# The last layer of a four-layer graph network: two matrix products folded, one residual product moved into the units, normalisation steps re-placed

## What is computed

```python
def _L3_gnn_ref(h, adj, W, a, W_res, gamma, beta):
    Wh = h @ W
    src = Wh @ a[:F_OUT]
    dst = Wh @ a[F_OUT:]
    e = jax.nn.leaky_relu(src[:, :, None] + dst[:, None, :], ALPHA)
    e = jnp.where(adj > 0, e, NEG_INF)
    attention = jax.nn.softmax(e, axis=-1)
    h_prime = jnp.einsum('bij,bjf->bif', attention, Wh)
    h_prime = h_prime + h @ W_res
    h_prime = jax.nn.elu(h_prime)
    mean = jnp.mean(h_prime, axis=-1, keepdims=True)
    var = jnp.var(h_prime, axis=-1, keepdims=True)
    return (h_prime - mean) * jax.lax.rsqrt(var + LN_EPS) * gamma + beta
```

## Time and profile before

| | us |
|---|---|
| three runs, lowest, median, highest | 3643.5, 3647.93, 3651.93 |
| the profiled execution | 3658.79 |
| its span, first to last instruction | 3656.9 |
| of it the last layer, from 3264.1 | 392.8 |

### The profile page before, as it was taken

How to read it: one execution, slowest core, us unless ns; L and a number is a source line. 1 busy time by engine, 2 the same in 40 slices (tenths; PEclk the granted TensorE clock), 3 DMA queues, 4 the chain that set the end, 5 groups by cost and what they waited for, 6 DMA issues and landing times. The chain is left out here.

```text
span 3656.9 us, 79212 instructions
## 1 busy us (share of the span) xinstructions
PE 3145.9 (86%) x31515; PEld 1741.2 (48%) x31515; DVE 3129.5 (86%) x4797; ACT 2982.5 (82%) x3625; POOL 1005.0 (27%) x565
## 2 busy tenths in 40 slices
PE   7996998999999869889898898988988989968885
PEld 5663666666666633333333333333333333336764
DVE  6665887888888779999999999999999999956666
ACT  5664887887788759999999999999999999956555
POOL 4432655655566610100000000000010000016554
PEclk9997999999999989999999999999999999988788
DMA  6540000000000000000000000000000000001111
GB/s 229 207 141 16 22 16 19 19 19 19 19 19 19 22 7 10 10 10 10 10 10 12 11 10 10 10 10 10 10 10 10 10 10 10 13 17 57 51 52 35
DMA packets 67251, 110.62 MB, mean 30 GB/s; under 512 B 25941, under 2 KB 25944, under 8 KB 66904
## 3 DMA queue, kind: packets, MB, share of 16 engines
q1 hardware_dynamic: 66904, 105.77, 9.3%
HBM read 86.87 MB, written 18.87 MB: 29 GB/s over the span
## 5 line engine op out<-in xcount | busy, mean ns | idle before, releaser
L980 ACT ACTIVATE l_scalar_ring<-l_w,l_r 128x1024 f32<-128x1024 f32 x1632 | 1712.9, 1141 | 34.8 <-DVE l_values L1026 25.7
L1094 DVE TENSOR_SCALAR l_vector_ring<-l_w_code,l_r_code 128x2048 f32<-128x2048 f32 x1232 | 1588.9, 1354 | 3.1 <-issue 0.2
L917 PE MATMUL scores<-l_scalar_ring,l_signs 128*32 128x512 f32 x6528 | 792.0, 604 | 91.2 <-ACT l_scalar_ring L980 90.9
L927 PE MATMUL scores<-l_vector_ring,l_signs_code 128*32 128x512 f16 x9856 | 670.9, 393 | 140.1 <-DVE l_vector_ring L1094 139.3
L242 ACT COPY probs_t<-turned 128x512 f32<-128x512 f32 x576 | 324.7, 587 | 422.5 <-PE turned L201 422.3
L433 POOL TENSOR_TENSOR l_masked<-l_relu,mask 128x1024 f32<-128x1024 f32 x256 | 546.2, 2134 | 438.0 <-ACT l_relu L585 397.1
L927 PEld LDWEIGHTS scores<-l_vector_ring,l_signs_code 128*32 128x32 bf16 x9856 | 243.1, 95 | 592.1 <-DVE l_vector_ring L1094 308.8
L212 PE MATMUL outT<-probs_t,l_values 128*64 128x128 f32 x6144 | 433.9, 284 | 88.3 <-ACT probs_t L242 40.3
L212 PEld LDWEIGHTS outT<-probs_t,l_values 128*64 128x64 f32 x6144 | 343.1, 140 | 234.2 <-DVE l_acc L667 104.4
L269 ACT ACTIVATE l_probs<-l_logits,negmax 128x1024 f32<-128x1024 f32 x384 | 443.7, 1155 | 6.6 <-DVE negmax L260 6.6
L201 PE MATMUL turned<-ident,l_probs 128*128 128x128 f32 x3072 | 436.6, 287 | 12.1 <-issue 7.3
(11 more groups left out here) (239 smaller groups left out, 3148.1 us busy)
## 6 DMA issues: line engine op xcount, KB each, us to landing
mask<-masks_kept SPq DMA_DIRECT2D x192, 256.0 KB, 2.6
l_adj<-adj SPq DMA_DIRECT2D x64, 512.0 KB, 5.6
masks_kept<-l_mask_ring SPq DMA_DIRECT2D x64, 256.0 KB, 4.2
x_res<-x SPq DMA_DIRECT2D x8, 256.0 KB, 5.1
out<-x_res SPq DMA_DIRECT2D x8, 256.0 KB, 2.8
l_w_both<-L_gnn_Wq SPq DMA_DIRECT2D x2, 64.0 KB
l_w_both<-L_gnn_Wk SPq DMA_DIRECT2D x2, 64.0 KB
l_w_both<-L_gnn_Wv SPq DMA_DIRECT2D x2, 64.0 KB
```

Source lines behind the costliest of these rows:

```text
L917: last = nc.tensor.matmul(s.scores[g * ROWS:(g + 1) * ROWS, buf, half, :], signs[:, window], scalar_ring[:, at % SCALAR_RING, g, halves[ha ...
L927: last = nc.tensor.matmul(s.scores[g * ROWS:(g + 1) * ROWS, buf, half, :], signs_code[:, par, g % 2, window], parts(vector_ring[:, at % VE ...
L980: last = nc.scalar.activation(scalar_ring[:, at % SCALAR_RING, g, :], w[:, par, :], ACT.Relu, bias=r[:, par, column:column + 1])
L1094: last = nc.vector.tensor_scalar(vector_ring[:, at % VECTOR_RING, g:g + 2, :], w_code[:, par, :, :], r_code[:, par, 0, column:column + 1], ...
```

## The change

- **W once through the attention vectors.** Ahead of the first graph, PE turns W, multiplies it by the dst half of a (repeated over 128 columns, `w_dst`) and by the src half (`w_src`). dst and src then come straight from hT; whT and its two fills are gone.
- **Rows of h as values.** `values` is relu(y) of the graph, made by DVE alone (`take_values`, L1481 of the new file, 128x512 from SBUF to SBUF, unit 5). W is applied where the output is turned: `unit_end` (L1392) multiplies `turned_both` by w, which stands twice, one above the other, so it adds the halves as well.
- **Residual per unit.** One more matmul (two instructions in the trace, since float32 runs as two) behind each unit's product, into columns 128 to 191 of `outT` (L1385). `copy_out` copies 192 columns instead of 128.
- **Five fills for nine**: 0 and 1 (hT), 2 and 3 (dst), 4 (src), one in each of units 0 to 4, always ahead of the product on PE and behind `copy_out` on DVE. ACT's copy of dst is gone: the relu reads `dst_slope` with a scale.
- **Norm steps.** The reciprocal stands before `copy_out` (`inverse_sum`). Input norm: centre and square on POOL in units 3 and 4, scale on DVE in 5, apply on POOL in 6. Output norm: centre in unit 2 and square in unit 5 on POOL, `out_seed` on DVE in 6; `out_scale` of graph b-2 in unit 0, its gamma on DVE in unit 3 and its `out_add` in unit 4. AHEAD is 4. SP's program is as it was (one more weight load).

The core of the diff:

```diff
-    K = 9
-    RING, AHEAD = 4, 5
+    K = 5
+    RING, AHEAD = 4, 4
...
             def out_centre(b):
 
-                centred, square, elu = (work[:, i, :, :] for i in range(3))
                 g.wait_ge(sems["out_mean"], b + 1)
-                nc.gpsimd.tensor_tensor(centred, elu, total[:, 1, :].unsqueeze(2).to_broadcast(shape), ALU.subtract
-                                        ).then_inc(sems["out_centred"], 1)
+                wait(g, sems["out_scaled"], b)
+                nc.gpsimd.tensor_tensor(work[:, 0, :, :], work[:, 2, :, :], total[:, 1, :].unsqueeze(2).to_broadcast(shape),
+                                        ALU.subtract).then_inc(sems["out_centred"], 1)
+
+            def out_square(b):
+
                 g.wait_ge(sems["out_centred"], b + 1)
-                nc.gpsimd.tensor_tensor(square, centred, centred, ALU.mult).then_inc(sems["out_square"], 1)
+                nc.gpsimd.tensor_tensor(work[:, 1, :, :], work[:, 0, :, :], work[:, 0, :, :], ALU.mult
+                                        ).then_inc(sems["out_square"], 1)
 
             def out_scale(b):
 
@@ -1314,98 +1322,117 @@
                 nc.gpsimd.tensor_tensor(work[:, 3, :, :], work[:, 0, :, :], total[:, 7, :].unsqueeze(2).to_broadcast(shape), ALU.mult
                                         ).then_inc(sems["out_scaled"], 1)
 
-            def graph(b, par, project, norm, first=False):
+            def graph(b, par, project, norm, before=2):
                 for n in range(NB):
                     if n + AHEAD < NB:
                         mask(b, par, n + AHEAD)
                     elif project:
                         mask(b + 1, 1 - par, n + AHEAD - NB)
-                    if n == 3 and not first:
+                    if n == 0 and before > 1:
+                        out_scale(b - 2)
+                    if n == 2 and before > 0:
                         out_centre(b - 1)
+                    if n == 3 and norm:
+                        layer_norm_centre(g, s, sems, next_norm(s, b), b + 2)
                     if n == 4 and norm:
-                        layer_norm_centre(g, s, sems, next_norm(s, b), b + 2)
-                    if n == 5 and norm:
                         layer_norm_square(g, s, sems, b + 2)
-                    if n == 6 and not first:
-                        out_scale(b - 1)
-                    if n == 7 and norm:
+                    if n == 5 and before > 0:
+                        out_square(b - 1)
+                    if n == 6 and norm:
+                        g.wait_ge(sems["values_ready"], b + 1)
                         layer_norm_apply(g, s, sems, next_norm(s, b), par, b + 2, b * K + 2)
...
             def fill(b, par, k):
                 bank = fill_bank(s, b, k)
-                wait_for_bank(pe, s, sems, b, K, k, 0 if k < 2 else 4 if 4 <= k < 7 else 2)
+                wait_for_bank(pe, s, sems, b, K, k, 0 if k < 2 else 2)
                 cols = slice((k % 2) * BANK, (k % 2 + 1) * BANK)
                 if k < 2:
                     pe.wait_ge(sems["y_ready"], b + 1)
                     last = turn_y(pe, s, par, k, bank)
                 elif k < 4:
-                    last = nc.tensor.matmul(bank[0:D, :], w[:], s.hT[:, cols], start=True, stop=True)
-                elif k < 6:
-                    last = nc.tensor.matmul(bank[:], a_dst[:], whT[:, cols], start=True, stop=True)
+                    last = nc.tensor.matmul(bank[:], w_dst[0:D, :], hT[0:D, par, cols], start=True, stop=True)
                 else:
                     for j in range(NB):
-                        nodes = slice(j * P, (j + 1) * P)
-                        if k == 6:
-                            out_, lhs, rhs = bank[:, j:j + 1], whT[:, nodes], acol[:, 0:1]
-                        else:
-                            out_, lhs, rhs = bank[:, j * D:(j + 1) * D], s.hT[:, nodes], (w if k == 7 else wres)[:]
-                        last = nc.tensor.matmul(out_, lhs, rhs, start=True, stop=True, skip_group_check=True)
+                        last = nc.tensor.matmul(bank[:, j:j + 1], hT[0:D, par, j * P:(j + 1) * P], w_src[0:D, :], start=True, stop=True,
+                                                skip_group_check=True)
                 last.then_inc(sems["fill_ready"], 1)
+
+            def product(par, n, u):
+
+                pe.wait_ge(sems["half0_copied"], STARTS + u + 1)
+                pe.wait_ge(sems["half1_copied"], STARTS + u + 1)
+                wait(pe, sems["out_copied"], STARTS + u)
+                for j in range(NB):
+                    half = j % 2
+                    nc.tensor.matmul(s.outT[half * D:(half + 1) * D, 0:P], values[:, par, j, :], s.probs_t[:, j, :],
+                                     start=(j < 2), stop=(j >= NB - 2), skip_group_check=True)
+                nc.tensor.matmul(residual, hT[0:D, par, n * P:(n + 1) * P], wres[0:D, :], start=True, stop=True,
+                                 skip_group_check=True).then_inc(sems["out_ready"], 1)
+
+            def unit_end(u):
+
+                pe.wait_ge(sems["out_copied"], STARTS + u + 1)
+                wait(pe, sems["unit_done"], STARTS + u)
+                nc.tensor.matmul(unit_out, turned_both[:, 0:P], w[:], start=True, stop=True, skip_group_check=True
+                                 ).then_inc(sems["out_turned"], 1)
 
             def graph(b, par, project, first=False):
                 for n in range(NB):
                     u = b * NB + n
-                    fills = list(range(fills_before(n), fills_before(n + 1))) if project else []
                     turn_probs(pe, s, sems, probs[:, n % 2, :], u)
                     if not (first and n == 0):
-                        turn_out(pe, s, sems, u - 1, 0, unit_out)
-                    for k in fills[:1]:
+                        unit_end(u - 1)
+                    for k in fills_at(n, project):
                         fill(b + 1, 1 - par, k)
                     wait(pe, sems["unit_done"], STARTS + u)
-                    probs_times_values(pe, s, sems, values[:, par, :, :], u)
-                    for k in fills[1:]:
-                        fill(b + 1, 1 - par, k)
+                    if n == 0:
+                        pe.wait_ge(sems["values_ready"], b + 1)
+                    product(par, n, u)
...
+            def take_values(b, par):
+
+                v.wait_ge(sems["y_ready"], b + 1)
+                nc.vector.tensor_scalar(values[:, par, :, :], s.y[:, par, :, :], 0.0, None, ALU.max
+                                        ).then_inc(sems["values_ready"], 1)
...
+            def out_gamma(b):
+
+                v.wait_ge(sems["out_scaled"], b + 1)
+                nc.vector.tensor_tensor(spread[:, 0, :, :], work[:, 3, :, :], gamma[:].unsqueeze(1).to_broadcast([P, NB, D]), ALU.mult)
+
...
-            def graph(b, par, project, norm, first=False):
+            def graph(b, par, project, norm, before=2):
                 for n in range(NB):
                     u = b * NB + n
-                    fills = list(range(fills_before(n), fills_before(n + 1))) if project else []
+                    v.drain()
                     if n > 0:
                         finish(par, n - 1, u - 1)
-                    elif not first:
+                    elif before > 0:
                         finish(1 - par, NB - 1, u - 1)
                     if n + 2 < NB or project:
                         logit((n + 2) % NB, u + 2)
-                    for k in fills[:1]:
+                    inverse_sum(n)
+                    v.wait_ge(sems["out_ready"], u + 1)
+                    nc.vector.tensor_copy(turned_both[:], s.outT[:, 0:P + D]).then_inc(sems["out_copied"], 1)
+                    for k in fills_at(n, project):
                         take_fill(b + 1, 1 - par, k)
-                    copy_out(v, s, sems, u)
-                    for k in fills[1:]:
-                        take_fill(b + 1, 1 - par, k)
-                    if n == 0 and not first:
+                    if n == 0 and before > 0:
                         elu(b - 1, 1 - par)
-                    if n == 1 and not first:
+                    if n == 1 and before > 0:
                         out_mean(b - 1)
                     if n == 2 and norm:
                         layer_norm_mean(v, s, sems, next_norm(s, b), b + 2)
-                    if n == 4 and not first:
+                    if n == 3 and before > 1:
+                        out_gamma(b - 2)
+                    if n == 4 and before > 1:
+                        out_add(b - 2)
+                    if n == 5 and norm:
+                        layer_norm_scale(v, s, sems, next_norm(s, b), b + 2)
+                    if n == 5 and project:
+                        take_values(b + 1, 1 - par)
+                    if n == 6 and before > 0:
                         out_seed(b - 1)
-                    if n == 7 and not first:
-                        out_add(b - 1)
-                    if n == 6 and norm:
```

(2 more changed lines are left out.)

144 lines of the change are left out of this document (71 added, 73 removed).

## The result

The changed kernel takes 3675.0 us (median of 10 runs, 3658.3 to 3682.1), the kernel before, beside it on the same chip, 3644.7. The ratio is 1.0074, with a 95% interval of 1.0060 to 1.0089: the change costs 0.74%. The forecast was 3609, with a range up to 3638. The profiled execution of the changed kernel took 3680.7, 60.7 more than the 3620.0 that the sum of the prediction gives for a profiled execution (3658.8 less 38.8).

The account below looks back on a forecast made before the run. No engine fills a graph; the PE-ACT loop, fills, DVE norm steps and clock set it. Graphs 2 to 5 -16.7, graph 6 -1.6, graph 1 -12.3, graph 0 -4.2, prologue -5.6, tail +1.6: -38.8 from 3647.9, 3609 us; range 3576 to 3638.

Parts of the forecast that it names:

- Prologue and tail: Ahead of graph 0: 5.6 us saved, mainly the whT fill and its copy; behind graph 7: 1.6 us added.
- The wait that the change makes: Masks queue on SP behind the store of graph b-2, delaying product 6: 4.95 us each in graphs 2 to 5.
- the price of 0.7: DVE's making of the values in unit 5, beside POOL: 0.7 us, with ends of 0.43 and 2.1.
- the sum at full clock: Product-to-product steps of a middle graph: 33.4 us without a wait on SP, 38.35 with it.
- 4.0 more for the clock: Half-speed PE work in each of graphs 2 to 5: 4.0 us, 2.1 of it in unit 6, bounds 1 and 9.
- the step 0 to 1: From product 0 to product 1: DVE has hT 0.68 and the ELU 0.95, giving 3.95 us.
- the foreseen stall: PE standing over 6 us before product 6 in graphs 2 to 5, then unit 6 at half speed, +2.1 us.
- the half clock takes over: Rival, 8%: all units at 1.2 GHz, a graph of 54 us, in all 3705, slower than before.
- a mean clock below 0.7: Sign in the new profile: the forecast is wrong if the graphs' mean clock falls below 0.7.
- The plain unit: A unit without a fill: the residual's two matmul instructions add 0.24 us to PE's loop, 3.48 to 3.72.
- Graph 6: No input norm there: 33.4 plus 2.5 for lateness and 2.3 for the clock, 38.2 us for 39.8.
- Graph 7: Plain units gain 0.24 us each, the addition that delayed its end goes: no change in length.

## Why the prediction was wrong

**Prologue and tail: right.** The first relu starts 7.0 earlier (3283.41 for 3290.37), the first `l_z` 7.7 earlier; 5.6 was forecast. The tail grew by 0.9 instead of 1.6.

**The wait that the change makes: right in place, slightly low in size.** Every link stood where the text put it: store behind the addition, mask behind the store, `l_base`, square, reduce, values, product 6, in graphs 2 to 5 and not in 6 (3.7 there). The step to product 6 took 9.35 to 9.52, where 3.9 + 4.95 = 8.85 was forecast. The addition came 1.0 later, since product and residual ran at half clock, and the scalar of the square's chain took 1.31 beside POOL instead of about 0.2. The values took 0.41 to 0.42 in all graphs, so the price of 0.7 was too high.

Product to product, one round of graph 4 against the sum at full clock:

| from, to | forecast | after |
|---|---|---|
| 1 to 2 | 5.45 | 6.0 |
| 2 to 3 | 3.9 | 6.7 |
| 3 to 4 | 4.6 | 8.2 |
| 4 to 5 | 4.05 | 5.4 |
| 5 to 6, with SP's wait | 8.85 | 9.5 |
| 6 to 7 | 3.72 | 5.7 |
| 7 to 0 | 3.8 | 5.3 |
| 0 to 1 | 3.95 | 7.5 |

The forecast had 4.0 more for the clock, 2.1 of it behind product 6. The excess of 16 lies mainly elsewhere: 3.6 in the step 0 to 1, and 7.1 in the three steps behind it.

**The step that failed: what DVE does while POOL is busy, in the step 0 to 1.** The prediction followed POOL's lateness to product 6 and stopped. It priced the ELU in the step to product 1 at 0.95 for both operations, although the row that it used for the values, `l_low` stretched to 1.36 by one `l_base`, was of this very kind. Here POOL's queue held two `l_base` in one piece at that place, and `l_high` lasted 2.34. The step to product 1 took 6.35 to 6.87 in graphs 2 to 6, forecast 3.95. Lateness from SP's wait is part of the reason: with the store moved the stall went in graphs 4 and 5 (steps of 4.7 and 4.6). It is not all of it, since graph 2 has the stall ahead of any wait of SP. What else puts two `l_base` together there stays open: in graph 2 the output norm's steps now in unit 0 stand ahead of them, but the kernel with only the addition a graph later, which has those steps in unit 6, held the ELU up as well. The idle matmuls, which nearly leave the waits as they are, give the miss without the clock: graphs of 44.1 for 38.35. That is 5.8 per graph at most, as that kernel's product 4 still ran at half clock behind the src fill (step to product 5: 6.0 for 4.05).

**The clock: right in kind, mis-sized by more than twice.** The term was 4.0 per graph (bounds 1 and 9). The changed kernel's 53.6 less the 44.1 with PE kept busy is 9.5, already above the upper bound; and the half clock was not mainly behind the foreseen stall but behind the unforeseen one, where 22 us follow at 0.50. The error in the reasoning: a unit of half speed was priced as a single unit, and the clock as coming back by itself. With a fill in each of units 2 to 4, PE at half clock has no gap at all there (22.00 busy in 22.00), and nothing hides its slower work: the steps 1 to 4 cost 6.0, 6.7 and 8.2. The rival "the half clock takes over" had 8% and gave a graph of 54: graphs 2, 4 and 5 took 54.1, 54.4 and 54.0. That the number fits is partly luck: it took all units at 1.2 GHz and no stall at the ELU, and the graphs had a mean clock of 0.65 and that stall. Its total of 3705 was too high, since graphs 0 and 1 stayed out of it. The row that should have raised its chance was at hand: four graphs of before stood at 0.73 to 0.80 without any wait of SP. The text's condition, a mean clock below 0.7, was met in four of the five graphs from 2 to 6.

The rule of the Trainium skill, "TensorE: Matmul & The Clock Gate", section "HAM oscillation — how this bites in real kernels", that waiting between bursts brings the half clock back each time, agrees with this: in graphs 2 to 5 both stalls (3.3 to 3.8 and 6.4 to 6.8 us) were followed by it. Falls that it does not cover stand further down.

**The plain unit: 3.72 forecast, 3.84 found.** From the start of a product to the next transposes it is 1.38 (3644.93 to 3646.31) where it was 1.03: the residual costs 0.36 in the loop (3.84 for 3.48), not 0.24. Two instructions of 64 columns with their own weights are not two sixteenths of a fill of 16 such. Over 64 units that is 8 us, and moving it away gave 8 to 25.

**Graph 6: 38.2 forecast, 49.8 found**; with the ELU freed alone it took 41.1, so 8.7 of the 11.6 can come from there. It is not sure: with the store moved as well it took 46.6, at a clock of 0.63. **Graph 7** rose by 3.4: 0.12 x 8 beyond the forecast plain unit is 1.0, and the stretch 3631.7 to 3662.7 has a clock of 0.82 where it was 0.92.

**What was right in the whole:** the folding. With the norm steps back it gave 27 us, and with the store moved, the residual ahead and the ELU freed the same change gives 52 us on the kernel before (3595.0 for 3647.2), more than the 39 of the forecast.

## What to carry to other kernels

When a step is moved later, look in every queue for what waits on it, and then follow the lateness past the first engine that feels it. Moving the waiting store behind work that is long finished was a small edit and worth 42 us, of which 16 (19 in graphs 2 to 5 alone) are the wait that the prediction saw, with the half clock behind it; the rest came through the ELU and the clock. Price again, too, every DVE operation that can now start while POOL is busy. A stall is not priced by its length alone: where the work behind it fills PE at half clock without a gap, here for 22 us, two operations held up by some 2 us cost 9.4 a graph.
